# A graph attention kernel: the third pair of rectified chunks is added on VectorE instead of in TensorE's products

## What is computed

```python
hs = (x @ Ws + bs).reshape(N, H, HD)
hd = (x @ Wd + bd).reshape(N, H, HD)
hs_e = hs[src]
e = jax.nn.leaky_relu(hs_e + hd[dst], SLOPE)
logits = jnp.einsum('ehd,hd->eh', e, attn)
m = jax.ops.segment_max(logits, dst, num_segments=N)
ex = jnp.exp(logits - m[dst])
s = jax.ops.segment_sum(ex, dst, num_segments=N)
alpha = ex / s[dst]
out = jax.ops.segment_sum(alpha[..., None] * hs_e, dst, num_segments=N)
```

## Time and profile before

| | |
|---|---|
| median of 3 runs | 2290.95 us (2289.56 to 2295.0) |
| profiled execution | 2295.07 us |
| its span, first to last instruction | 2293.2 us |
| busy: PE, DVE, ACT, POOL | 2142.6, 1670.7, 1122.0, 770.8 us |
| mean granted TensorE clock | 0.974 |

### The profile page before, as it was taken

One profiled execution on the slowest core, in us unless ns is written; L12 is line 12 of the kernel. 1 busy time (PEld: TensorE's weight loads), 2 busy tenths in 40 slices (PEclk: granted clock), 3 DMA queues, 4 the chain that ended last, 5 costly groups with the idle time before them and its releaser, 6 DMA issues. The chain is left out here.

```text
span 2293.2 us, 91571 instructions
## 1 busy us (share of the span) xinstructions
PE 2142.6 (93%) x32341; PEld 1718.5 (75%) x32342; DVE 1670.7 (73%) x4413; ACT 1122.0 (49%) x2757; POOL 770.8 (34%) x798
## 2 busy tenths in 40 slices
PE   5999998999899999999997899899999999999578
PEld 3665554555799999999996556589999999999457
DVE  5223996344688888888888774488888888888873
ACT  1101210014566666666664324466666666666463
POOL 0000001111455555555553001255555555554000
PEclk9999999999999999999998899999999999999789
DMA  5000223323788888888884024488888888887301
GB/s 189 0 1 8 79 96 87 112 94 96 217 252 250 250 252 251 252 250 250 251 251 155 33 85 120 126 243 251 251 251 251 250 248 251 252 240 241 132 22 47
DMA packets 139237, 397.61 MB, mean 173 GB/s; under 512 B 21705, under 2 KB 76268, under 8 KB 139124
## 3 DMA queue, kind: packets, MB, share of 16 engines
q0 software_dynamic: 59584, 298.64, 43.1%
q1 hardware_dynamic: 76525, 90.41, 12.6%
q10 hardware_dynamic: 3044, 7.45, 1.0%
HBM read 368.18 MB, written 16.78 MB: 168 GB/s over the span
## 5 line engine op out<-in xcount | busy, mean ns | idle before, releaser
L498 ACT ACTIVATE at_relu<-at_turned,ah_attn_size 128x512 f32<-128x512 f32 x1092 | 719.3, 696 | 432.7 <-PE at_turned L557 431.4
L479 POOL DMA_INDIRECT at_rows<-table,ah_index x360 | 360.7, 1002 | 296.0 <-DVE ah_index L681 104.0
L479 POOL DMA_INDIRECT ah_room<-table,ah_index x352 | 351.7, 999 | 292.8 <-DVE ah_index L681 123.4
L555 PE MATMUL at_turned<-ah_place,dst_rows 96*128 96x128 bf16 x2208 | 401.2, 223 | 19.8 <-issue 9.6
L557 PE MATMUL at_turned<-ident,ah_room 128*128 128x128 f32 x2208 | 416.6, 279 | 0.0
L557 PE MATMUL at_turned<-ident,at_rows 128*128 128x128 f32 x2160 | 403.4, 277 | 1.4 <-issue 1.4
L555 PE MATMUL at_turned<-at_place,dst_rows 96*128 96x128 bf16 x2160 | 388.9, 222 | 0.0
L677 DVE SCALAR_TENSOR_TENSOR sums<-sums,at_factor,at_total 128x97 f32 x1456 | 343.8, 309 | 9.1 <-issue 6.0
L557 PEld LDWEIGHTS at_turned<-ident,ah_room 128*128 128x128 f32 x2208 | 317.6, 144 | 24.6
L557 PEld LDWEIGHTS at_turned<-ident,at_rows 128*128 128x128 f32 x2160 | 308.1, 143 | 24.1 <-issue 1.7
L667 DVE TENSOR_TENSOR at_spread<-at_lined,at_weight 128x1024 f32<-128x1024 f32 x182 | 223.0, 1225 | 132.4 <-ACT at_weight L508 119.3
(11 more groups left out here) (318 smaller groups left out, 3198.1 us busy)
## 6 DMA issues: line engine op xcount, KB each, us to landing
at_flags<-run_flags SPq DMA_DIRECT2D x182, 64.0 KB
dst_rows<-pr_parts SPq DMA_DIRECT2D x76, 144.0 KB, 2.6
ah_place<-local_rows SPq DMA_DIRECT2D x92, 96.0 KB
at_place<-local_rows SPq DMA_DIRECT2D x90, 96.0 KB
table<-ah_room SPq DMA_DIRECT2D x20, 400.0 KB, 2.4
ah_room<-table,ah_index POOLq DMA_INDIRECT x368
at_rows<-table,ah_index POOLq DMA_INDIRECT x360
mx_w<-in_L_mix_W_qkv SPq DMA_DIRECT2D x2, 2304.0 KB, 18.8
```

What stands on the lines that cost most here:

```text
L479: pool.indirect_dma_start(rows[b][:, j, :], None, table, bass.IndirectOffsetOnAxis(index[b][:, j:j + 1], 0)).then_inc(gathered[b], 16)
L498: act.activation(relu[c][:], turned[chunk(b, c)][:], ACT.Relu, scale=attn_size[:, c:c + 1]).then_inc(bent, 1)
L555: pe.matmul(into, dst_rows[:, bass.ds(at[j], 1), c * P:(c + 1) * P].rearrange("p o d -> p (o d)"), place[b][:, j * P:(j + 1) * P], start=T ...
```

## The change

Chunks 4 and 5 become a third joined pair: VectorE adds them with the relative sign, and TensorE has three products for the heads (twelve matmuls, was sixteen). VectorE's joins are also placed anew: pairs (2, 3) and (4, 5) of macro `head` stand where pairs (0, 1) and (2, 3) stood, at the head of the slot, and pair (0, 1) is now joined one slot earlier, as macro `turn`, behind `build_place` and ahead of `spread_out`. `slot` on VectorE gets `turn` as a new first argument. `pair_sign` of the third pair comes from the same loop over `JOINED`.

```diff
-JOINED, ALONE = ((0, 1), (2, 3)), (4, 5)
+JOINED = ((0, 1), (2, 3), (4, 5))
...
                     for j in range(G):
                         pe.matmul(head_row(j), rows[b][:, j, D + 1::QUAD], ident[:], start=True, stop=False)
-                    for c in ALONE:
-                        pe.wait_ge(bent, m * KC + (BANKS + c + 1))
-                        for j in range(G):
-                            pe.matmul(head_row(j), sign_mask[:, c, :], relu[c][:, j * P:(j + 1) * P], start=False, stop=False)
                     for k, (_, c) in enumerate(JOINED):
                         pe.wait_ge(joined, m * len(JOINED) + (k + 1))
...
-                def join(m):
-                    for from_, c in JOINED:
+                def join(m, pairs):
+                    for from_, c in pairs:
                         dve.wait_ge(bent, m * KC + (BANKS + c + 1))
                         dve.scalar_tensor_tensor(relu[c][:], relu[from_][:], pair_sign[:, c:c + 1], relu[c][:], ALU.mult, ALU.add).then_inc(joined, 1)
...
-                def slot(head, message, after=None, fresh=False, more=False):
+                def slot(turn, head, message, after=None, fresh=False, more=False):
...
                     if head:
                         line_up(head[0], fresh)
-                        join(head[0])
+                        join(head[0], JOINED[1:])
...
                     if after:
                         build_place(*after)
+                    if turn:
+                        join(turn[0], JOINED[0:1])
                     if head:
                         spread_out(head[0], head[1])
...
-                        slot(macro(i, b + 1), macro(i, b), macro(i, b + 3), more=True)
+                        slot(macro(i, b + 2), macro(i, b + 1), macro(i, b), macro(i, b + 3), more=True)
```

More of the change, by code:

```diff
@@ L714, in _ @@
                 step(dve.tensor_scalar(single[:], single[:], -FAR, None, ALU.mult))
-                slot(None, None, macro(0, 2))
-                slot(macro(0, 0), None, None, fresh=True)
+                slot(macro(0, 0), None, None, macro(0, 2))
+                slot(macro(0, 1), macro(0, 0), None, fresh=True)
                 with dve.Fori(0, LOOPS) as i:
                     for b in range(UNROLL):
-                        slot(macro(i, b + 1), macro(i, b), macro(i, b + 3), more=True)
-                slot(macro(LOOPS, 1), macro(LOOPS, 0))
-                slot(macro(LOOPS, 2), macro(LOOPS, 1))
+                        slot(macro(i, b + 2), macro(i, b + 1), macro(i, b), macro(i, b + 3), more=True)
+                slot(macro(LOOPS, 2), macro(LOOPS, 1), macro(LOOPS, 0))
+                slot(None, macro(LOOPS, 2), macro(LOOPS, 1))
                 dve.wait_ge(scanned, NM * SCANS + SCANS)
@@ L735, in _ @@
                 dve.sem_inc(merge_ready, 1)
-                slot(None, macro(LOOPS, 2))
+                slot(None, None, macro(LOOPS, 2))
                 at = places_of(nc, mybir.EngineType.DVE, block_of, 0, 1)
```

## The result

The changed kernel takes 2356.62 us (median of 4 runs, 2356.11 to 2357.63), the kernel before beside it 2292.97 us: a ratio of 1.0278 [1.0265, 1.0291], 64 us slower. The forecast was 2367.

The account below looks back on a forecast made before the run. TensorE was taken to set the pace at 7.20 us a slot; a wait for ScalarE would make it 7.62, and 0.42 us by 180 slots is +76 us, a median of 2367 us. Range 2318 to 2395.

Parts of the forecast that it names:

- The change adds a wait, not only work: VectorE's join (4, 5) waits for bend 5, ScalarE's last operation, with adds, copy, scans and `shifted` queued behind.
- The circle: From the load of `shifted` over chunk 4, bend 5, join (4, 5), adds and scans to the next load: 7.62 us.
- T: Start of TensorE's weight load of `shifted` in `turn_back`, from which the forecast counts times within a slot.
- stall: VectorE's idle time before join (4, 5), waiting for bend 5: 0.59 us a slot.
- the last signal: From the end of `shifted` on VectorE to TensorE's next load of it: taken as 0.09 us.
- What is hidden: Loop branch, `messages` products, their totals and POOL's gathers fit into slack and add nothing to the slot.
- the branch: Loop branch stopping TensorE's weight loads in one of four slots: 0.28 us, said to fall into slack.
- TensorE stays the bound: Rival: TensorE still sets the pace or the slot falls to 7.04 us, about 2268 us; chance 0.05.
- VectorE's bare chain: VectorE's own work for one slot with the added join and no waits: 7.04 us.
- It balances: Rival: the stall covers only what TensorE and the branch give back, slot 7.16 to 7.24, 2284 to 2298 us; chance 0.05.
- The clock falls: Rival: TensorE's idle 0.67 us a slot lowers its clock, kernel near 2810 us; chance 0.03.

Follow-up runs that it names:

- e5_no_bend5_wait: Changed kernel with the third join and third product using chunk 2, so nothing waits for bend 5 (chunks 4 and 5 left out of the logits): 2273.47 us, 0.9918.
- e3_three_at_head: Changed kernel with all three joins at the head of the slot, pair (0, 1) not moved: 2355.18 us, 1.028 of the kernel before.
- e4b_product_left_out_again: Second run of the kernel before without chunk 4's heads product, VectorE untouched: 2272.22 us beside 2289.88, 0.9917.
- e1_bend5_first: Changed kernel with bend 5 ahead of the factors in ScalarE's order: 2321.49 us, 1.0126 of the kernel before.
- e4_product_left_out: Kernel before without chunk 4's heads product (chunk 4 left out of the logits), VectorE untouched: 2514.41 us beside 2549.86, 0.9862.
- e7_four_in_one: Kernel before with pairs (0, 1) and (2, 3) added into one, chunks 4 and 5 with own products: 2571.9 us (1.0091) in group B, 2279.84 us (0.9955) in A.
- e2_join_behind_four: Changed kernel with join (4, 5) behind the first four of VectorE's eight adds: 2419.23 us, 1.0551 of the kernel before.

## Why the prediction was right

- **The change adds a wait, not only work.** Right, and shown: without the wait, with the same work, the kernel is faster than before (`e5_no_bend5_wait`); with it and join (0, 1) put back it is as slow as the change (`e3_three_at_head`).
- **The circle.** Each step is near its forecast: T to the end of chunk 4 1.76 (1.78 forecast), bend 5 done at T + 3.67 (3.70), join at T + 3.70 (3.73), stall 0.53 against its own queue's due time, 1703.14 + 0.665 (0.59), 3.13 to `shifted` (3.14). The slot is 7.56, not 7.62.
- **The size, 2367 for 2357.** The mis-sized term is the last signal, `shifted` to TensorE: taken as 0.09, between 0.05 and 0.12, it is 0.05. The row that gave 0.12 names `issue` as what ended its idle time, not `shifted`, so it didn't measure that signal. With about 0.02 less in the other steps that is 0.06 x 180 = 11 of the 12 us by which 76 exceeded 64. The kernel before, 2293 beside the change where the forecast had 2291, took 2 us of the miss back by chance.
- **What is hidden.** Right: slots with the branch are as long as the others; `messages` at T + 2.52; adds at T + 4.38, where the totals alone would let them start at 3.79 (1.27 after 2.52); joins 746 ns; each heads product 0.22 us (0.66 for three).
- **TensorE stays the bound.** Not borne out: busy 380 of 400 us. The rule of the Trainium skill, Perfetto Trace Analysis, section "Identifying the Most-Contended Engine", taken alone, promised 40 us. Where its premise was tried by itself (`e4b_product_left_out_again`) it gave 18, since circles of 6.97 and 6.99 us over VectorE stand right behind TensorE's 7.13. And with the third join's work but no wait (`e5_no_bend5_wait`) the ordinary slot is VectorE's bare chain, 7.01 (forecast 7.04), the branch isn't hidden (mean 7.10), and the time is 2273, near this rival's 2268.
- **It balances.** It needed a path shorter by 0.4 us. Taking 0.36 off the path to bend 5 (`e1_bend5_first`) still left 29 us of loss, since the factors became late.
- **The clock falls.** Not borne out: 1.00 in the loop, with weight loads idle 0.58 us in each ordinary slot. The oscillation of the Trainium skill, TensorE: Matmul & The Clock Gate, section "A second HAM failure mode: psum-queue depth-cycling", didn't come.

## What to carry to other kernels

Before work is moved off the busiest engine, ask for what the new instruction waits, and what stands behind it in its queue: here 0.22 us saved on TensorE a macro cost 0.36, because the last result of ScalarE came to stand ahead of VectorE's adds and scans. Sum each circle over the engines (from one instruction round to itself in the next iteration), the second longest too, since it caps what an edit can give: TensorE, 99% busy with 7.13 us a slot, stood here beside circles of 6.97 to 6.99. If a value comes last, let the engine that needs it latest wait for it, and feed a further join with values that are long done.

## What the runs showed of the hardware

The same kernel took 2290 to 2293 us in three groups and 2549 to 2550 us in the other two, with a spread of 0.5% or less in each. Each group of experiments ran on a chip of its own (those of A on chips 4 and 8, those of B on 0 and 12; the chip of the first pair isn't recorded), so the chip and the occasion can't be told apart. In group B the trace shows TensorE's weight loads stopping in the midst of a product, with nothing to wait for. From `e4_product_left_out` in B, the stretch, two rows of weight loads, and the two largest waits of its weight loads there:

```profile
1600.00:2000.00 400.00, 371.50 (x6971) 310.28 (x6971) 309.02 (x860) 235.29 (x618) 216.54 (x191) 1.00 0.73 213
```

```profile
1860.64 0.11 PEld L573 LDWEIGHTS at_heads<-at_relu,ah_sign_mask 128*8 128x8 f32 x3 [0.63 <-issue]
1861.37 0.35 PEld L573 LDWEIGHTS at_heads<-at_relu,ah_sign_mask 128*8 128x8 f32 x13 [0.62 <-issue]
```

```profile
PEld at_heads L573 <- issue: 26.9, 45, 0.6
PEld at_total L591 <- issue: 16.3, 34, 0.6
```

The kernel before in group A has 5.0 us in 14 times of the second kind in that stretch, its longest 0.4, and none of the first. The granted clock is 1.00 in both. The stops belong to places in the code: from 1700 to 1800 us of `e4_product_left_out` there are 24 of over 0.25 us in some 12 slots, and counted in weight loads the same pattern comes back, mostly within three loads, after 589 and again after 587; one pass of the loop, four slots, has 588. The gaps look as if TensorE's instructions came late, which isn't shown; why, and why in some groups only, is open. Their price is large: all comparisons of group B were of another balance, and `e7_four_in_one` changes sign with it. I had not expected either that an add could start no sooner than 1.27 us after the first of the 64 loads for the totals, though it waits only for the first half of them (`e2_join_behind_four`, with the totals as releaser). In the rows of VectorE's queue the wait for that half ends 0.97 after the first load (1705.95), and the add starts 0.30 after it (1706.25).
